# A graph network's history of scanned rows: one store of seven rows becomes two, of four and of three

## The reference

```python
def _pna_conv(x, src, dst, deg, avg_log, W_pre, b_pre, W_post, b_post, W_lin, b_lin):
    xi = x @ W_pre[:Fin]
    xj = x @ W_pre[Fin:]
    h = xi[dst] + xj[src] + b_pre
    mean = jax.ops.segment_sum(h, dst, N) / degc
    mean_sq = jax.ops.segment_sum(h * h, dst, N) / degc
    std = jnp.sqrt(jax.nn.relu(mean_sq - mean * mean) + EPS_VAR)
    mx = jax.ops.segment_max(h, dst, N)
    mn = jax.ops.segment_min(h, dst, N)
    agg = jnp.concatenate([mean, mx, mn, std], axis=-1)
    out = jnp.concatenate([agg, agg * amp, agg * att], axis=-1)
    out = jnp.concatenate([x, out], axis=-1) @ W_post + b_post
    return out @ W_lin + b_lin
```

## Time and profile before

| | us |
|---|---|
| time, median of 3 runs (lowest, highest) | 2560.24 (2541.18, 2604.75) |
| profiled execution, its own time | 2550.3 |
| its span, first to last instruction | 2547.9 |
| mean granted clock of PE, as a share | 0.884 |
| PE busy | 1757.2 (69%) |
| DVE busy | 1738.2 (68%) |
| POOL busy | 1003.5 (39%) |
| ACT busy | 443.1 (17%) |

### The profile page before, as it was taken

The page is one execution under the profiler, slowest core; times in us unless marked ns, Lnnn a source line. Parts: engine busy times, 40 slices in busy tenths (PEclk is TensorE's granted clock), DMA queues, the critical chain, the costliest instruction groups (busy, mean ns, idle before and its releaser), DMA issues.

```text
span 2547.9 us, 35959 instructions
## 1 busy us (share of the span) xinstructions
PE 1757.2 (69%) x12224; PEld 1161.4 (46%) x12224; DVE 1738.2 (68%) x4556; ACT 443.1 (17%) x1031; POOL 1003.5 (39%) x916
## 2 busy tenths in 40 slices
PE   0047777776796578898898753846787888887355
PEld 0025455445596245455555531523454555555233
DVE  4989999996504866676676652877665666666438
ACT  2035455552001001011010100200010101101002
POOL 2800000000400466666656564035565556556540
PEclk9999999998798788898899975978898889898677
DMA  3202222321351455555555432044454555444320
GB/s 85 58 26 99 105 95 94 106 110 74 98 179 32 130 176 181 169 189 176 187 175 181 166 120 89 15 140 141 157 190 156 170 164 188 155 168 153 132 82 26
DMA packets 148821, 327.18 MB, mean 128 GB/s; under 512 B 51083, under 2 KB 102604, under 8 KB 148314
## 3 DMA queue, kind: packets, MB, share of 16 engines
q1 hardware_dynamic: 95674, 159.39, 18.5%
q10 hardware_dynamic: 23152, 104.77, 11.6%
q0 software_dynamic: 29872, 61.49, 8.6%
HBM read 172.44 MB, written 153.12 MB: 128 GB/s over the span
## 4 chain that ended last, share of the span: by engine, by line
DVE 39%; PE 26%; another core or an unknown queue 11%; issue 11%; POOL 6%; DMA 6%; SPq 1%; ACT 1%; DVEq 0%; ACTq 0%; POOLq 0%
DVE scanned L1517 11%; PE ps L1047 10%; PE ps L1128 8%; POOL scanned L980 6%; DVE scanned L1901 4%; DVE scanned L1897 4%; DVE scanned L1514 3%; DMA scanned<-table,rest_idx 2%; DMA A<-counts 2%; PE ps L1182 2%; DVE accs L1867 2%; PE ps L1112 2%; PE ps L1235 2%; DVE accs L1849 1%
## 5 line engine op out<-in xcount | busy, mean ns | idle before, releaser
L980 POOL DMA_INDIRECT scanned<-table,rest_idx x784 | 852.2, 1087 | 826.7 <-issue 338.0
L1047 PE MATMUL ps<-big,A 125*128 125x128 bf16 (+1 forms) x7500 | 732.7, 252 | 131.5 <-issue 109.0
L1047 PEld LDWEIGHTS ps<-big,A 125*128 125x128 bf16 x7500 | 600.6, 100 | 270.3 <-issue 174.2
L1128 PE MATMUL ps<-S,big 126*128 126x500 bf16 (+3 forms) x2100 | 499.5, 390 | 190.9 <-DVE accs L1849 79.2
L1128 PEld LDWEIGHTS ps<-S,big 126*128 126x128 bf16 (+1 forms) x2100 | 205.2, 106 | 438.6 <-issue 173.8
L1849 DVE TENSOR_TENSOR accs<-accs,ps 128x1000 f32<-128x1000 f32 (+1 forms) x154 | 166.7, 1082 | 312.2 <-remote 246.9
L1897 DVE SCALAR_TENSOR_TENSOR scanned<-scanned,rest_neg 128x128 f32<-128x128 f32 x784 | 271.3, 346 | 73.7 <-DMA scanned<-table,rest_idx 65.0
L1517 DVE TENSOR_SCALAR scanned<-scanned 128x400 bf16<-128x400 f16 x1000 | 312.1, 386 | 0.0
L1059 PE MATMUL ps<-scanned 128*128 128x400 bf16 x1000 | 212.4, 344 | 116.3 <-DVE scanned L1517 107.9
L1901 DVE SCALAR_TENSOR_TENSOR scanned<-scanned,rest_neg 128x128 f32<-128x128 f32 x784 | 271.0, 346 | 0.0
L997 POOL IOTA Y<- 128x784 int32 x1 | 0.8, 782 | 503.2 <-DVEq L1705 503.2
(11 more groups left out here) (305 smaller groups left out, 1427.5 us busy)
## 6 DMA issues: line engine op xcount, KB each, us to landing
rest_history<-scanned SPq DMA_DIRECT2D x112, 896.0 KB
A<-counts ACTq DMA_DIRECT2D x75, 800.0 KB
S<-picks SPq DMA_DIRECT2D x60, 640.0 KB
picks<-S ACTq DMA_DIRECT2D x25, 800.0 KB, 3.4
counts<-A ACTq DMA_DIRECT2D x25, 800.0 KB, 3.4
scanned<-table,rest_idx POOLq DMA_INDIRECT x784
scanned<-records SPq DMA_DIRECT2D x200, 7.5 KB, 1.7
table<-Y SPq DMA_DIRECT2D x10, 320.0 KB, 2.5
```

Of the source, the lines that this page charges most:

```text
L980: nc.gpsimd.indirect_dma_start(out=rows[:, w, s, :], out_offset=None, in_=tables[1 + l], in_offset=bass.IndirectOffsetOnAxis(ap=rest_idx[: ...
L1047: m = nc.tensor.matmul(acc[:, bank, 0:width], A[0:NB, slot, a, :], XS[0:NB, a, c, 0:width], start=a == 0 and c == 0, stop=a == NT - 1 and ...
L1128: m = nc.tensor.matmul(ps[:, bank + h, 0:len(blocks) * NB], XS[0:rows, a, c, 0:F], pick[0:rows, n % RING, 0:len(blocks), a % PART, 0:NB], ...
```

## The change

The store of a window is cut in two: rows 0 to 3 leave when the eighth operation of the window is done, rows 4 to 6 when the fourteenth is. Each part adds 16 to the same semaphore, so those who wait for it (DVE before it reuses the buffer, POOL before it reads the history) wait for twice the count. The pieces of one partition are 4 KB and 3 KB.

```diff
+STORED = [(0, 4), (4, WIN)]
...
                     for k in SCANNED[s]:
                         n, w = l * WINDOWS + k, k % 2
-                        sp.wait_ge(main.scan_ops, 2 * WIN * (n + 1))
-                        sp.dma_start(hist_rest[:, k * WIN * 2 * F:(k + 1) * WIN * 2 * F],
-                                     histf[:, w * WIN * 2 * F:(w + 1) * WIN * 2 * F])\
-                            .then_inc(main.stored[w], 16)
+                        for s0, s1 in STORED:
+                            sp.wait_ge(main.scan_ops, 2 * (WIN * n + s1))
+                            sp.dma_start(hist_rest[:, (k * WIN + s0) * 2 * F:(k * WIN + s1) * 2 * F],
+                                         histf[:, (w * WIN + s0) * 2 * F:(w * WIN + s1) * 2 * F])\
+                                .then_inc(main.stored[w], 16)
...
-                finish_scan(main, l, 16 * (WINDOWS // 2) * (l + 1), rest_history, P * REST, fixI[:, 1:2], restI)
+                finish_scan(main, l, 16 * len(STORED) * (WINDOWS // 2) * (l + 1), rest_history, P * REST, fixI[:, 1:2], restI)
...
                 if n > 1:
-                    dve.wait_ge(main.stored[w], 16 * (n // 2))
+                    dve.wait_ge(main.stored[w], 16 * len(STORED) * (n // 2))
```

## The result

On the chip of the first series the median went from 2598.01 us (22 runs, 2540.48 to 2638.57) to 2615.11 us (22 runs, 2575.49 to 2652.61): a ratio of 1.0098, 95% interval 1.0052 to 1.0144. The base had moved too: 2560.24 was the median of three runs, and with 22 it is 38 us higher, more than the upper half of the predicted range. On the five other chips that the experiments met, the kernel before needs 2274 to 2282 us, and on the four of them where it ran as it is the same change is faster: 0.9877 to 0.9963 in five comparisons.

What follows compares the result with a forecast made beforehand. In the scan stages no engine was full: PE, DVE and POOL took turns holding up the next slot. Terms -2.2 (layer ends) and -5 (stages) sum to -7.2 us, so 2560.24 becomes 2553.0 us; range 2532 to 2588.

Steps and rivals of the forecast that it cites:

- (1): SP's 112 more DMA issues and waits: cost 0, hidden by its standing still; at most 35.8 us without that cover.
- (3): Last store of each layer: lands 1.1 us sooner, twice, so -2.2 us, between -1.8 and -2.6.
- (5): Stores reading `hist` while DVE writes its later rows: taken as 0, at most +15 us in 112 windows.
- (2): Bytes and descriptors: runs of 4 and 3 KB for 7 KB add at most 0.40 us of latency, no engine cost.
- (4): Scan stages: first part moves in idle DMA time, shortening seven long gather landings on the chain; -5 us, bounds -9.0 to 0.
- the sign of being right: In the scan stages, gathers that follow a store directly would land in 6 us or less.
- each transfer keeps the rings for its fixed part: Rival: in the DMA queues, 1.30 us of start and completion is occupied time; +88 us, 2648, slower; chance 0.07.
- the parts leave together: Rival: SP comes late to the first wait, so both issues follow each other; 2560; chance 0.07.
- the nameless waits: DVE's waits ahead of L1849 for a releaser the profile can't name: 246.9 us in 43 places.
- the nameless waits are congestion: Rival: queues behind the stores hold up PE or its signals; 43 waits shrink by 1.28 us each, 2503, faster; chance 0.06.
- the nameless waits changed by tens of us: Sign of being wrong: DVE's waits without a named releaser would change by tens of us.
- hidden anyway: Rival: scan-stage landings shorten, but PE or the nameless wait holds the next slot; only both layer ends gain, 2558; chance 0.30.

Runs made afterwards that it cites:

- two_late: The changed kernel with both parts of the store waiting for the whole window, so no early first part: 2274.15 us, 0.9938 of the kernel before.
- null: The kernel before, unchanged, run against itself on another chip than the first series: 2284.12 us over six runs.
- two_again: The changed kernel as it is, run again on another chip than the first series: 2263.41 us, 0.9877 of the kernel before.
- pe_: Matmuls of one bank of `select` done twice, in the kernel before (one store) and the changed kernel (two): 2378.05 and 2369.19 us.
- burst_: Matmuls of one bank run seven times in every third slot, in the kernel before (one store) and the changed kernel (two): 2576.94 and 2572.62 us.
- two_third: The changed kernel as it is, run a third time, on yet another chip: 2264.18 us, 0.9948 of the kernel before.

## Why the prediction was right and wrong

**Right.** (1), the instructions: 224 issues of 320 ns in SP's idle time; two_late, which has them all and no lead, is level with before over two chips (+0.8, standard error 2.1), though its scan stages are 8 us longer in both profiles, so a small cost of the second transfer isn't excluded. (3), the last store: 3.54 us became 2.30, 1.24 saved where 1.1 was taken and 2.26 to 2.66 us were the ends. (5), reading `hist` while DVE writes: +2 ns on 346, nothing. (2) holds as far as seven parts with runs of 1 KB a partition are faster still, so short runs aren't paid for here. And where gathers bind, (4) has the right sign and about the right size: -5 us was forecast for the stages, and the profiles of the five chips show 6 less (1139.0 and 1133.3) with 5 less of DVE's wait for rows. For the whole it was -7.2, and -11.3 was measured at equal clock. That the size fits so well is partly luck: it was added up from seven landings on another chip's chain, where null has eleven of over 4 us and the change doesn't bring them all to 6 us or less (7.86 in two_again), as the sign of being right had it.

**The rivals.** That each transfer keeps the rings for its fixed part, with +88 us, is refuted: seven transfers in place of one are the fastest. That the parts leave together is refuted by the 1.57 to 1.58 us between them in every window; two_late is that rival made by hand. That the nameless waits are congestion is not borne out: they did not shrink with the split, in layer 1 at the same clock they are 181.0 and 190.0 us, and on five chips with the same stores they are absent. The Trainium skill's fixed 2.0 us and bytes at 436 GB/s ("DMA: Bandwidth & Descriptors", section "Anatomy of one DMA") are a fit for transfers that GpSimd issues, which the prediction doesn't say; these stores are issued by SP. The fit gave estimates of 4.10, 2.90 and, for a part of 128 KB, 2.30 us; measured were 3.52 to 3.54, 2.30 and 1.69, so for these stores its slope held and its constant was about 0.6 us too long. The Trainium skill's advice of 1 MiB or more per transfer (same page, section "Rules for kernel authors") is given there for bandwidth, and it is the rule that speaks against this change; on the five chips it points the wrong way, since the data of a large transfer come into being row by row and the first rows could have gone. The three chances of the prediction's outcomes add up to 1.01, a slip without effect.

**Wrong.** The forecast was faster by 0.3%, and on the first chip it is slower by 1.0% (0.5 to 1.4), 62 us above the forecast time. Two steps failed. The first is the base, and it is the larger: the median of three runs, 2560.24, was carried over as if it stood, with a range from the spread of three; 22 runs gave 2598.01, 38 us more, with two of those three among its four lowest. The second is the sum's assumption that the stage would get term (4)'s -5 us and that nothing else would move: the nameless waits, 11% of the chain, stood in it at nothing, with no term in the sum and nothing upward in its range. The prediction took them for waits "for something without a name", although the kernel's own waits say that L1849 can only wait for PE; and it gave "the nameless waits changed by tens of us" as a sign of being wrong, which came true, 308 to 366 us. The rival "hidden anyway" named them as next and still let them stand as they were. What the runs showed in place of -7.2 is +17 us between the medians on this chip (13 to 37 by the interval of the ratio), while the same change gains 11 where those waits are absent. That the stores caused the 58 us isn't shown: most of it lies in layer 0, at a lower clock, and in layer 1 the stage is 2 us shorter.

**Open.** Why the change costs 17 us on the first chip, where it saves 11 elsewhere, isn't settled. Only the first chip's traces have waits for late events, on DVE and on ACT (the largest 384.1 us before, 376.3 after), and PE's idle time by no releaser is also larger there (156 times, 109.0 us at L1047 before and 131.0 at L1050 after; in null that line's idle time from all releasers is 23.1). More work on PE (pe_) and work in bursts (burst_) don't turn the sign, but neither delays an event after its matmul. One candidate remains, which was only argued: in the changed kernel's 22 runs there the time goes with the granted clock, from about 2577 us at 0.878 to 2653 at 0.846, so two series whose clocks fell differently could differ by 17 us without the stores. The two layers of the profiled pair speak for it; the clocks of before's runs there are known for one execution alone (0.884, 2550.3 us). The interval, which excludes 1, speaks against plain chance, but not against clocks that differed between the two sets of runs; that no run of the changed kernel was under 2575 us, where eight of before's 22 were, is the stronger objection. That the late events themselves answer to the number or the timing of the stores is the other candidate. No later run met that chip, so neither could be tried.

## What to carry to other kernels

A store that waits for a whole window, while its first rows are long done, can be cut so that the first part moves in time in which the DMA engines stand idle; the gain is in who queues behind it (here gathers), it comes from the lead and not from the number of parts, and with more PE in the chain it was not seen in DVE's wait for them. Before pricing an edit of 0.3%, ask whether the base is known to 0.3%: three runs weren't enough, and one kernel differed by 14% from chip to chip. And where a tenth of the chain ends at a releaser that the profile can't name, read in the kernel which semaphores that instruction waits for and who raises them, and give it a bound in the sum, to both sides. A profiled pair is to be compared stage by stage with the clock beside it: here one layer had lost 74 us and the other nothing.

## What the runs showed of the hardware beyond this

- The same program took 2598 us on one chip and 2274 to 2282 on five others. In the profiles 234 of 269 us of the difference lie in the two scan stages (1423 and 1189 us), where DVE is busy equally long (461.6 and 461.4 us in layer 0) and waits for events of PE's that come 1.5 us or more after the recorded matmul. Those waits are absent on the five. The clock has a part too: 0.88 and 0.93 in layer 0's stage, PE busy 540.6 and 497.7 us for the same 3225 matmuls.
- Some gathers on POOL that are in progress while DVE runs its chain of operations are stretched, and each of these ends 0.8 us after the last of them; here one takes 2.84 us in place of 0.94, and the next start that much later. In two_third 84 gathers that began in a window were stretched, and 162 began and ended in one at their usual length, as the first below does. What decides between them isn't shown. The timeline of two_third (start, us, engine, line):

```profile
1087.57 1.03 POOL L983 DMA_INDIRECT scanned<-table,rest_idx  x1 [0.30 <-issue]
...
1088.91 2.84 POOL L983 DMA_INDIRECT scanned<-table,rest_idx  x1 [0.30 <-issue]
...
1090.59 0.34 DVE L1904 SCALAR_TENSOR_TENSOR scanned<-scanned,rest_neg 128x128 f32<-128x128 f32 x1
```

- A part of 512, 384 or 128 KB needs the same 320 ns (median) to issue as the whole of 896 KB, and 784 stores in place of 112 bring no loss that can be measured.
